# Attention in split bf16 on one Trainium2 core: heads expanded by eight transfers of 72 rows instead of twelve of 24

## The reference

```python
# x: (32, 256, 128) float32; 16 heads of 8 columns
y = layernorm(x) * ln_w + ln_b
q, k, v = y @ wq, y @ wk, y @ wv                 # for each head
weights = softmax(causal(q @ k.T / sqrt(8)))
a = concat(weights @ v) @ wo + x
x1 = _layernorm(x + a)                           # without weights
f = x1 @ W.T + b + x1 @ (up_aux @ (lora_up @ (lora_down @ down_aux))).T
out = _layernorm(x1 + f)
```

## Time and profile before

| | |
|---|---|
| median of 3 runs | 437.6 us (436.97 to 439.66) |
| the profiled execution, its own time | 438.39 us |
| its span, first to last instruction | 436.7 us |
| mean granted TensorE clock | 0.989 |
| PE busy | 418.1 us (96%) |
| DVE, ACT, POOL busy | 87%, 78%, 71% |
| the 16 DMA engines on SP's queue | 59.2% |

### The profile page before, as it was taken

One profiled execution on the slowest core, in us unless ns is written; L12 is line 12 of the kernel. 1 busy time (PEld: TensorE's weight loads), 2 busy tenths in 40 slices (PEclk: granted clock), 3 DMA queues, 4 the chain that ended last, 5 costly groups with the idle time before them and its releaser, 6 DMA issues.

```text
span 436.7 us, 15760 instructions
## 1 busy us (share of the span) xinstructions
PE 418.1 (96%) x5571; PEld 335.9 (77%) x5571; DVE 381.4 (87%) x1056; ACT 342.1 (78%) x865; POOL 308.0 (71%) x395
## 2 busy tenths in 40 slices
PE   7698999999999999999999999999999999998994
PEld 3366677888888888888888888888888888877762
DVE  4589978999999999999999999999999999988664
ACT  2376777788888888888888888888888888887871
POOL 6764857777777777777777778777777777754763
PEclk9699999999999999999999999999999999999998
DMA  2566576665775667666676666666676676555111
GB/s 77 151 171 170 152 190 148 164 169 155 196 192 164 180 173 175 179 174 165 176 194 176 171 166 178 173 173 169 161 193 183 170 176 175 147 140 137 42 49 38
DMA packets 77915, 69.16 MB, mean 158 GB/s; under 512 B 9307, under 2 KB 68530, under 8 KB 77874
## 3 DMA queue, kind: packets, MB, share of 16 engines
q1 hardware_dynamic: 76446, 67.68, 59.2%
q10 hardware_dynamic: 1428, 0.95, 0.9%
HBM read 47.07 MB, written 21.00 MB: 156 GB/s over the span
## 4 chain that ended last, share of the span: by engine, by line
PE 84%; DVE 5%; DMA 4%; SPq 2%; ACT 2%; issue 2%; POOL 0%; POOLq 0%; ACTq 0%; DVEq 0%
PE pv_bank L1363 20%; PE score_bank L1344 12%; PE bank L1376 11%; PE bank L1371 8%; PE max_bank L1330 7%; PE max_bank L1326 6%; PE max_bank L1331 6%; PE score_bank L1345 6%; PE bank L1433 3%; PE bank L1434 3%; DVE rowmax L1042 2%; DMA kx<-k_rows 2%; PE score_bank L1420 1%; DMA q_rows<-parts 1%; ACT qx L670 1%
## 5 line engine op out<-in xcount | busy, mean ns | idle before, releaser
L1042 DVE TENSOR_REDUCE rowmax<-max_bank 128x2 f32<-128x512 f32 (+1 forms) x384 | 245.8, 675 | 16.5 <-PE max_bank L1331 8.8
L615 ACT ACTIVATE probs<-score_bank 128x384 f32<-128x384 f32 x512 | 222.3, 491 | 39.1 <-PE score_bank L1345 26.5
L512 POOL TENSOR_SCALAR_AFFINE_SELECT probs<-probs 128x1024 f32<-128x1024 f32 x127 | 137.8, 1095 | 56.6 <-ACT probs L615 56.4
L1344 PE MATMUL score_bank<-qx,kx 74*128 74x256 bf16 x512 | 119.9, 273 | 0.5 <-DMA qx<-mT 0.5
L1345 PE MATMUL score_bank<-qx,kx 74*128 74x128 bf16 x512 | 101.6, 218 | 0.0
L1363 PE MATMUL pv_bank<-probs,v_ext 128*32 128x256 f32 x2032 | 97.5, 329 | 0.0
L1330 PE MATMUL max_bank<-kx,qx 128*128 128x128 bf16 x512 | 86.6, 221 | 2.3 <-DVE rowmax L1042 2.3
L1331 PE MATMUL max_bank<-kx,qx 74*128 74x128 bf16 x512 | 86.2, 220 | 0.0
L1363 PEld LDWEIGHTS pv_bank<-probs,v_ext 128*32 128x32 f32 x2032 | 56.3, 109 | 31.9 <-issue 6.8
L1330 PEld LDWEIGHTS max_bank<-kx,qx 128*128 128x128 bf16 x512 | 48.6, 98 | 15.0 <-issue 5.9
L1344 PEld LDWEIGHTS score_bank<-qx,kx 74*128 74x128 bf16 x512 | 49.7, 97 | 6.5 <-issue 1.6
(11 more groups left out here) (123 smaller groups left out, 615.7 us busy)
## 6 DMA issues: line engine op xcount, KB each, us to landing
kx<-k_rows SPq DMA_DIRECT2D x187, 96.0 KB
qx<-q_rows SPq DMA_DIRECT2D x128, 96.0 KB
qx<-q_rows SPq DMA_DIRECT2D x64, 104.0 KB
q_rows<-parts SPq DMA_DIRECT2D x32, 192.0 KB, 2.2
k_rows<-parts SPq DMA_DIRECT2D x31, 192.0 KB, 2.4
xa<-in_x SPq DMA_DIRECT2D x32, 128.0 KB, 3.9
xr<-in_x SPq DMA_DIRECT2D x32, 128.0 KB, 2.3
out<-y SPq DMA_DIRECT2D x32, 128.0 KB, 3.4
```

What stands on the lines that cost most here:

```text
L512: pool.affine_select(out=t, in_=t, compare_op=ALU.is_ge, fill=0.0, base=0, pattern=[[0, GROUP * NB], [1, P]], channel_multiplier=-1)\
L615: act.activation(probs[:, h, 0:PW], score_bank[SCORE_BANK[h]][:, 0:PW], ACT.Exp, scale=SCALE / Q_SCALE)\
L1042: dve.tensor_reduce(to, of, AX.X, ALU.max).then_inc(s_mread[unit], 1)
L1344: pe.matmul(b[:, 0:SEQ], k[0:SCORE_ROWS, i, 0:P], q[0:SCORE_ROWS, i, :], start=True, stop=True)
```

## The change

A batch's queries and keys are expanded in eight transfers instead of twelve: four sets of four heads, one transfer of all 72 query rows and one of all 72 key rows each. A row now has 2048 bytes. The source is a hand-made access pattern on the DRAM buffer. For queries its outer dimension is 3 with stride 0 (the same 24 rows three times), for keys 3 with a stride of 8 times 16 rows; inside it lie 24 rows of 4 times 256 elements. Each set has a semaphore, and units 0, 3, 6 and 9 of the maxima wait for their own set. The zeros no longer lie in DRAM: one more transfer per batch, `clear_max_rows`, writes partitions 72 and 73 from `zero_rows` in SBUF and counts in the first set's semaphore. The two parts of the maxima load in one transfer. The first batch's transfers change in the same way. SP waits for each set of the batch before, ahead of the transfers of that set.

```diff
+SETS = 4
+SET = HEADS // SETS
...
-        q_rows = [nc.dram_tensor(f"q_rows{i}", [(PART_ROWS + MAX_PARTS) * HEADS, SEQ], BF16).ap() for i in range(2)]
+        q_rows = [nc.dram_tensor(f"q_rows{i}", [PART_ROWS * HEADS, SEQ], BF16).ap() for i in range(2)]
...
-        EXPAND = 16 * 2 * PARTS
+        EXPAND = [16 * 3] + [16 * 2] * (SETS - 1)
         STORES = 16 * 2
-        MAX_ROWS = 16 * MAX_PARTS
+
+        def heads_of(number):
+            return slice(number * SET, number * SET + SET)
+
+        def queries_of(number, parity):
+            t = q_rows[parity]
+            return bass.AP(tensor=t.tensor, offset=number * SET * SEQ,
+                           ap=[[0, PARTS], [HEADS * SEQ, PART_ROWS], [1, SET * SEQ]])
+
+        def keys_of(number, parity):
+            t = k_rows[parity]
+            return bass.AP(tensor=t.tensor, offset=number * SET * SEQ,
+                           ap=[[HD * HEADS * SEQ, PARTS], [HEADS * SEQ, PART_ROWS], [1, SET * SEQ]])
...
+            def clear_max_rows(slot):
+                sp.dma_start(qx[slot][SPLIT_ROWS:SCORE_ROWS, :, :], zero_rows[:, :]).then_inc(s_expand[0], 16)
+
             def expand(it, o):
...
                 sp.wait_ge(s_score[HEADS - 1], it.done(o - RING))
                 alone(sp, "sp")
-                sp.wait_ge(s_expand[0], it.done(o - 1, EXPAND))
...
-                for half in range(HALVES):
-                    heads = slice(half * HALF, half * HALF + HALF)
-                    if half == 0:
+                sp.wait_ge(s_expand[0], it.done(o - 1, EXPAND[0]))
+                r, p = it.ring(o), it.parity(o)
+                clear_max_rows(r)
+                for number in range(SETS):
+                    if number == 0:
                         sp.wait_ge(s_q_stored, it.done(o, 16))
                     else:
-                        sp.wait_ge(s_expand[1], it.done(o - 1, EXPAND))
-                    for turn in range(PARTS):
-                        a, n = turn * PART_ROWS, PART_ROWS + (MAX_PARTS if turn == PARTS - 1 else 0)
-                        sp.dma_start(qx[r][a:a + n, heads, :], q[0:n, heads, :]).then_inc(s_expand[half], 16)
-                    if half == 0:
+                        sp.wait_ge(s_expand[number], it.done(o - 1, EXPAND[number]))
+                    sp.dma_start(qx[r][0:SPLIT_ROWS, heads_of(number), :], queries_of(number, p))\
+                        .then_inc(s_expand[number], 16)
+                    if number == 0:
                         sp.wait_ge(s_stored, it.done(o, STORES))
-                    for turn in range(PARTS):
-                        a = turn * PART_ROWS
-                        sp.dma_start(kx[r][a:a + PART_ROWS, heads, :],
-                                     k[turn * HD:turn * HD + PART_ROWS, heads, :]).then_inc(s_expand[half], 16)
+                    sp.dma_start(kx[r][0:SPLIT_ROWS, heads_of(number), :], keys_of(number, p))\
+                        .then_inc(s_expand[number], 16)
...
             def load_max_rows(it, o):
                 sp.wait_ge(s_mT, it.done(o))
-                for part in range(MAX_PARTS):
-                    sp.dma_start(qx[it.ring(o)][SPLIT_ROWS + part:SPLIT_ROWS + part + 1, :, :],
-                                 mT[part * HEADS:(part + 1) * HEADS, :]).then_inc(s_mrow, 16)
+                sp.dma_start(qx[it.ring(o)][SPLIT_ROWS:SCORE_ROWS, :, :], mT[:, :]).then_inc(s_mrow, 16)
...
-                if unit % (UNITS // HALVES) == 0:
-                    pe.wait_ge(s_expand[unit // (UNITS // HALVES)], it.done(o, EXPAND))
+                if unit % (UNITS // SETS) == 0:
+                    number = unit // (UNITS // SETS)
+                    pe.wait_ge(s_expand[number], it.done(o, EXPAND[number]))
```

More of the change, by code:

```diff
@@ L267, in load_weights @@
                     sp.dma_start(tile[:, :], dram[:, :]).then_inc(s_w, 16)
[L269 to L272, removed]
             def load_xa(it, o):
@@ L287, in store_parts @@
                 if it.static:
-                    sp.wait_ge(s_expand[0], it.done(o - 2, EXPAND))
-                    sp.wait_ge(s_expand[1], it.done(o - 2, EXPAND))
+                    for number in range(SETS):
+                        sp.wait_ge(s_expand[number], it.done(o - 2, EXPAND[number]))
                 p3 = it.done(o)
@@ L326, in store_first_queries @@
             def store_first_queries():
                 sp.wait_ge(s_p3q, 1)
[L328 to L347, removed]
+                sp.dma_start(q_rows[0].rearrange("(i p) s -> p i s", p=P), parts[:, :, 0, :]).then_inc(s_q_stored, 16)
+            def expand_first_queries():
+                sp.wait_ge(s_zero, 1)
+                sp.wait_ge(s_slot[0], 2)
+                clear_max_rows(0)
+                sp.wait_ge(s_q_stored, 16)
+                for number in range(SETS):
+                    sp.dma_start(qx[0][0:SPLIT_ROWS, heads_of(number), :], queries_of(number, 0))\
+                        .then_inc(s_expand[number], 16)
@@ L655, in store_first_keys, with expand_first_keys @@
                                   parts[:, 0:n, 1, :]).then_inc(s_stored, 16)
[L657 to L666, removed]
+            def expand_first_keys():
+                act.wait_ge(s_slot[0], 2)
+                act.wait_ge(s_stored, STORES)
+                for number in range(SETS):
+                    act.dma_start(kx[0][0:SPLIT_ROWS, heads_of(number), :], keys_of(number, 0))\
+                        .then_inc(s_expand[number], 16)
             def fill_queries(slot):
@@ L726, in first @@
                 copy_v(at, 0)
-                expand_first_keys(0)
-                expand_first_keys(1)
+                expand_first_keys()
                 first_parts(at, 1)
@@ L1338, in scores @@
                 if h == 0:
-                    pe.wait_ge(s_mrow, it.done(o, MAX_ROWS))
+                    pe.wait_ge(s_mrow, it.done(o, 16))
                 last = last_in_bank(h)
```

16 lines of the change are left out of this document (5 added, 11 removed).

## The result

The changed kernel takes **728.8 us** (median of 4 runs, 727.3 to 730.3), the kernel before on the same chip 438.0 (4 runs). The ratio is 1.663, with a 95% interval of 1.657 to 1.670. The forecast was 740, in a range of 640 to 900.

What follows compares the result with a forecast made beforehand. TensorE bounds the kernel before; three confined DMA engines would bound the changed one. A batch takes 17.1 + 4.05 + 0.4 = 21.55 us; 16.0 + 689.6 + 35.0 gives a span of 740.6, forecast 740 us, range 640 to 900.

Steps and rivals of the forecast that it cites:

- Engines from the counts: Expansions: largest number up to 16 dividing both sides' outermost counts gives 3 engines, always the same; 4475 packets under 512 bytes.
- rival A: Expansions: the 72 rows decide, or more engines share each transfer; TensorE stays the bound, 436.4 us; chance 0.10.
- E: Expansions: only the zero-stride queries are confined, keys run on 12 engines; 535 us; chance 0.02.
- Pace of the loaded engines: Loop, on engine 0: expansions at 23.0 GB/s, other transfers and idle time make 21.55 us a batch.
- the other two terms: Per batch on the loaded engines: 4.05 us for other transfers at 18.2 GB/s, and 0.4 us idle.
- rival C: Expansions: three engines, but at the slow rate of 16.4 GB/s, 28.45 us a batch; 962 us; chance 0.05.
- the other argument: Rate of one engine: three engines meet less competition than twelve, so 23.0 GB/s was taken, 17.1 us a batch.
- The sum: Whole span: start 16.0, 32 batches at 21.55 = 689.6, end 35.0; span 740.6 us.
- Rival D: Loop: TensorE at 1.2 GHz all the way becomes the bound again, up to 24.4 us a batch; 833 us; chance 0.09.
- the 9 that I wrote: Loop: PE waits about 9 us a batch for expanded keys or queries.
- What gets cheaper: SP's issues: three fewer at 0.38 us and one load of maxima fewer save 1.5 us a batch, hidden, worth nothing.
- Maxima that wait for their own heads: Maxima units could start three transfers earlier; worth something only where PE waited for keys, 1.4 us in all.

Runs made afterwards that it cites:

- e9: Kernel before, with eight of a batch's twelve expansions read from a source written as 3 times 8 rows: 572.0 us.
- e7: Kernel before, with eight of a batch's twelve expansions read from a source written as 4 times 6 rows: 500.1 us.
- e8: Kernel before, with eight of a batch's twelve expansions read from a source written as 6 times 4 rows: 491.8 us.
- e1: Changed kernel with the two outer source dimensions exchanged, 24 rows outermost, for queries and keys: 449.0 us, ratio 1.025.
- e11: e1 with two sets of eight heads instead of four of four, so four expansions of 72 rows by 4096 bytes: 437.9 us, ratio 1.002.
- e6: Kernel before with only the load of maxima changed, one transfer instead of two: 436.6 us, ratio 0.998.

## Why the prediction was right, and where it wasn't

**Engines from the counts.** Right, and exact: 4475 as forecast. The same rule gives the count of each of the eleven experiments, with 3, 4, 6 and 12 engines for expansions, and in the changed kernel, e9, e7 and e8 the numbers of packets in flight agree. That it is always the same three engines, on which the time rests, is what the three packets in flight bear out. Rivals A and E are refuted. The Trainium skill (DMA: Bandwidth & Descriptors, "Why a DMA increments its semaphore by 16 and not by 1") states this rule, and all of these counts agree with it.

**Pace of the loaded engines.** 17.1 + 4.05 + 0.4 = 21.55 us were forecast, 21.2 to 21.3 came. The single packet records give the term that counts: a packet of 2048 bytes lasts 90 ns in the mean, 22.7 GB/s (23.0 was taken), and 192 of them an engine and batch make 17.3 us. So the other two terms together are about 4.0 instead of 4.45: 144 pieces of 512 bytes at 27 ns are 3.9, and next to no idle time is left. But the way to the 23.0 was partly luck. It was read from one stretch of 1 us, where rows of 4096 bytes took 162 ns. Between 60 and 370 us of the kernel before they took 249 ns in the mean, 16.4 GB/s. So rival C's price was the rate of such rows while twelve engines ran at once, and the sentence against it, that the earlier trace rows speaks against it, picked a good moment. What decided was the other argument, that three engines meet less competition: in e9 such rows take 159 ns in the median, against 240 before.

**The sum.** The last wait for maxima ends at 690.5, and 36.0 us remain (35.0 forecast). The first expansions are issued at 13.6 instead of 14.5, so they move from about 15.1 on, and 32 batches took 675.4, 21.1 each. Against the forecast that is -0.9, -14.2 and +1.0: 726.6 for 740.6.

**The clock.** Rival D had it half right: with pauses in every period the granted clock went back and forth between 1.2 and 2.4 GHz, 0.82 in the mean of the loop. PE's work a batch grew from 12.2 to 404.58 / 27.3 = 14.8 us, which is 12.2 / 0.82. It stayed below 21.3, so in the loop it cost nothing. It is why PE waits 6.4 us a batch and not the 9 that I wrote.

**What gets cheaper.** This step was wrong. I priced three issues less at 1.5 us saved, by the 0.38 us of the old form. In e1, where the queues are not backed up, the expansions and the clearing issue in 6.26 + 0.69 us against 4.37: 2.6 us more, of which the single load of maxima gives 0.4 back. SP had only 1.8 to spare, so some 0.4 us a batch are missing, and the period grew from 12.2 to 12.7. In the changed kernel this lies under the engines and moved nothing. But rival A, which is e1's kernel in all but name, was priced at 436.4 and is 449.0. Had the engines been twelve, the forecast would have said no change where e1 loses 2.5%, because an instruction in a new form was costed by the row of the old one and no upper bound was set for it.

**Maxima that wait for their own heads.** Never seen by itself, since each run with four sets has the issues of four sets too. e11, with two sets, and e6, with the old halves, are within 0.3% of before, and the waits of the earlier trace rows bound what finer ones could give.

## What to carry to other kernels

Write down the outermost count of both sides of every transfer, and take the largest number up to 16 that divides both: in every run here it is the number of DMA engines, and transfers on three engines shared the same three. A mean DMA share of 0.3 can hide three full engines; landing times of bystanders that grow, issues longer than their twins, and the number of packets in flight point to them. Then add up the issuing engine's issues, waits and rest over one period before trusting that fewer transfers are cheaper: the price is by the transfer and its form, not by the byte.

## What the runs showed of the hardware

- **An issue costs by form.** Expansions with equal counts on both sides: 0.36 to 0.46 us in the median of a kernel, with rows of 2048 or 4096 bytes. Unequal ones: 0.68 to 0.84 us (72 against 3 x 24 or 24 x 3 rows; 24 against 3 x 8 and 6 x 4, about 0.70), and 0.61 for 24 against 4 x 6. The maxima took 0.57 us for one part and 0.69 for both. That the inequality is the cause, and not the number of dimensions in the source, isn't separated: every unequal transfer here has one more. And equal counts alone don't make an issue cheap: one part of the maxima has 16 pieces on both sides, and stores of parts (128 on both sides, two or three pieces in each) take 0.38 to 0.52 us.
- **Exchanging two outer dimensions** in a source moved 280 us, with the same bytes, rows and piece sizes.
- **A packet is slower when more engines run.** 4096 bytes took 240 ns in the median with mostly twelve in flight, and 159 in e9, where it was mostly three.
- **Two limits that lie close give a period longer than either.** e7 has an engine load of 13.5 us by my sum and SP's work of 13.4; its period is 14.3, with waits of 0.9 us, most of them for the store.
